# A selective-scan stage with whole scans in place of half scans, bf16 parts made ahead of their transfers, and another order in the experts' stage

## The reference, cut to what matters

```python
# experts, summed with the gate's weights w
h = relu(bn(einsum('bfd,edh->bfeh', x, W1) + b1)); h = relu(bn(einsum('bfeh,ehk->bfek', h, W2) + b2))
y = einsum('bfed,fe->bfd', einsum('bfeh,ehd->bfed', h, Wo) + bo, w)
# Mamba: 128 channels, 32 states for each channel, one step for each token
h = h * exp(dt_t[:, :, None] * A) + (dt_t * u_t)[:, :, None] * B_t[:, None, :]
y = einsum('bds,bs->bd', h, C_t)
```

## Time and profile before

| what | us |
|---|---|
| median of the timed runs (three, 1082.22 to 1087.21) | 1083.85 |
| the profiled execution's own time | 1080.03 |
| its span, first to last instruction | 1077.9 |
| PE, DVE, ACT, POOL busy in the span | 841.7, 799.9, 513.3, 541.9 |
| experts' stage, about 341.7 to 417 | 75 |
| scan stage, 499.5 to 965.1 | 465.6 |

### The profile page before, as it was taken

One profiled execution on the slowest core, in us unless ns is written; L12 is line 12 of the kernel. 1 busy time (PEld: TensorE's weight loads), 2 busy tenths in 40 slices (PEclk: granted clock), 3 DMA queues, 4 the chain that ended last, 5 costly groups with the idle time before them and its releaser, 6 DMA issues.

```text
span 1077.9 us, 11533 instructions
## 1 busy us (share of the span) xinstructions
PE 841.7 (78%) x3813; PEld 356.6 (33%) x3813; DVE 799.9 (74%) x1054; ACT 513.3 (48%) x1015; POOL 541.9 (50%) x356
## 2 busy tenths in 40 slices
PE   7873665768766997985897877887887887888897
PEld 4441344647634332431121111111111111114575
DVE  1249998866433333378999999999999999985465
ACT  1365300284352665574555555555554444436521
POOL 0010749410100000014999999999999999880100
PEclk9987855687565999895657578567567557559866
DMA  9000001600100000001110111011011011000001
GB/s 389 37 0 0 1 0 34 138 1 1 59 1 0 2 1 1 1 15 35 36 43 16 27 43 27 16 43 34 12 40 41 12 33 43 1 0 1 1 15 28
DMA packets 20505, 33.09 MB, mean 31 GB/s; under 512 B 10078, under 2 KB 19294, under 8 KB 19422
## 3 DMA queue, kind: packets, MB, share of 16 engines
q1 hardware_dynamic: 20446, 32.36, 10.6%
HBM read 17.57 MB, written 1.20 MB: 17 GB/s over the span
## 4 chain that ended last, share of the span: by engine, by line
PE 39%; DVE 31%; issue 13%; ACT 11%; POOL 4%; SPq 1%; DMA 1%; DVEq 0%; ACTq 0%; POOLq 0%
DVE pair_arrays L1617 13%; DVE pair_arrays L1601 5%; PE PS L748 4%; PE PS L720 4%; ACT pair_arrays L895 3%; PE PS L730 3%; PE PS L420 3%; PE PS L574 3%; ACT PS L895 3%; PE PS L840 2%; PE PS L510 2%; DVE pair_arrays L1423 2%; ACT token_weights L895 2%; PE PS L866 2%; PE PS L293 1%
## 5 line engine op out<-in xcount | busy, mean ns | idle before, releaser
L1257 POOL TENSOR_TENSOR pair_arrays<-pair_arrays 128x736 f32<-128x736 f32 x192 | 332.5, 1749 | 24.8 <-DVE pair_arrays L1617 24.5
L895 ACT ACTIVATE PS<-PS,A_negative 128x368 f32<-128x368 f32 x384 | 191.6, 538 | 129.6 <-PE PS L730 129.3
L1617 DVE TENSOR_TENSOR_SCAN pair_arrays<-PS,scan_carry,pair_arrays 128x368 f32<-128x368 f32 x256 | 235.8, 964 | 0.3
L1601 DVE TENSOR_TENSOR pair_arrays<-pair_arrays,PS 128x736 f32<-128x736 f32 x144 | 129.0, 896 | 8.8 <-PE PS L720 8.6
L748 PE MATMUL PS<-pair_arrays,weights 128*32 128x368 f32 x768 | 132.5, 715 | 1.5 <-POOL pair_arrays L1257 1.4
L1211 POOL TENSOR_TENSOR big<-pair_arrays 128x1104 f32<-128x1104 f32 (+15 forms) x32 | 55.8, 1762 | 131.5 <-DVE pair_arrays L1374 68.5
L1617 DVE TENSOR_TENSOR_SCAN pair_arrays<-PS,pair_arrays 128x368 f32<-128x368 f32 x128 | 110.3, 905 | 2.1 <-ACT PS L895 2.1
L720 PE MATMUL PS<-spread_rows,token_weights 96*128 96x368 bf16 x192 | 64.3, 428 | 37.9 <-DVE pair_arrays L1601 23.5
L1265 POOL TENSOR_TENSOR pair_arrays<-pair_arrays,token_weights 128x736 f32<-128x736 f32 x48 | 84.2, 1754 | 18.5 <-ACT token_weights L895 18.5
L720 PE MATMUL PS<-pair_arrays,token_weights 96*128 96x368 bf16 x192 | 71.7, 471 | 26.1 <-DVE pair_arrays L1601 19.8
L481 PE MATMUL PS<-big,weights 128*128 128x368 f32 (+15 forms) x192 | 62.8, 493 | 31.5 <-DVE big L1434 20.5
(11 more groups left out here) (190 smaller groups left out, 1246.3 us busy)
## 6 DMA issues: line engine op xcount, KB each, us to landing
big<-in_x SPq DMA_DIRECT2D x4, 2048.0 KB, 17.5
big<-decay_rows SPq DMA_DIRECT2D x4, 1104.0 KB, 15.7
spread_rows<-pair_arrays SPq DMA_DIRECT2D x96, 46.0 KB, 1.9
pair_arrays<-pair_arrays SPq DMA_DIRECT2D x96, 46.0 KB, 1.9
spread_rows<-big SPq DMA_DIRECT2D x48, 46.0 KB, 1.9
pair_arrays<-big SPq DMA_DIRECT2D x48, 46.0 KB, 1.9
weights<-in_wts SPq DMA_DIRECT2D x1, 2204.0 KB, 18.0
big<-in_wexp SPq DMA_DIRECT2D x1, 1536.0 KB, 7.6
```

Of the source, the lines that this page charges most:

```text
L895: return nc.scalar.activation(o, i, fn, **kw)
L1257: nc.gpsimd.tensor_tensor(hcbuf[t % NRING], hbuf[t % NRING], c4(seg).unsqueeze(1).to_broadcast([128, 2, G]), ALU.mult).then_inc(s("hc_read ...
L1601: tt(bx[t % NRING], b4(seg).unsqueeze(1).to_broadcast([128, 2, G]), PS[:, 2:4, 0:G], ALU.mult).then_inc(s("b_used"), 1)
L1617: nc.vector.tensor_tensor_scan(hbuf[t % NRING][:, h, :], PS[:, 4 + 2 * (t % 2) + h, 0:G], bx[t % NRING][:, h, :], carry[:, a:a + 1] if k e ...
```

## The change

**Parts.** ScalarE now makes the first bf16 part of each array (`first_part`) and the second from GpSimd's first remainder (`middle_part`); GpSimd writes the third as bf16 itself. The transfers copy bf16 rows, half the bytes, into one buffer that holds both segments' stacks, and the matmuls read them without a stride. SyncE waits for the four copies too.

**Scan.** One scan instruction does both halves of a step (`scan`). The 736 columns become 738: each half has a column ahead of it, in which the decay is 0 and the input is the carry, or 0. The halves lie next to each other across two banks (`decay_line`). The carry column is written by ScalarE (`carry_in`), two steps ahead. On VectorE the scan of step t - 1 comes behind the input product of step t. Eight small memsets clear the columns first.

**Experts.** TensorE does layer 1 of n + 1 ahead of layer 2 of n, and ScalarE the first activation of n + 1 ahead of the second of n.

```diff
-        stack = [[a.rearrange("p (j t) -> p j t", j=NJ) for a in two]
-                 for two in ((stack_own[:, 0], stack_own[:, 1]),
-                             (P1.rearrange("p a t -> p (a t)")[:, 0:NJ * G], P10.rearrange("p a t -> p (a t)")[:, 0:NJ * G]))]
+        stack = [[stack_own[:, a].bitcast(BF16)[:, i * NJ * G:(i + 1) * NJ * G].rearrange("p (j t) -> p j t", j=NJ)
+                  for a in range(2)] for i in range(2)]
...
+        def decay_line(t):
+            return PS[:, 4 + 2 * (t % 2):6 + 2 * (t % 2), :].rearrange("p b c -> p (b c)")[:, 512 - G1:512 + G1]
...
@@ SyncE
                 sp.wait_ge(s("rest_ready"), seg + 1)
+                sp.wait_ge(s("parts_moved"), 4 * (seg + 1))
...
-                    for part, rows in enumerate((at(1 + a, seg), rest[a][0], rest[a][1])):
+                    for part, rows in enumerate(parts16[a]):
@@ TensorE
             for n in range(NX):
+                if n + 1 < NX:
+                    layer1(n + 1)
                 layer2(n)
                 if n + 1 < NX:
-                    layer1(n + 1)
                     spread_weight(n + 1)
...
-                                            high(stack[seg % 2][1][0:3 * DB, 2 * (i % 2) + h]), start=True, stop=True)
+                                            stack[seg % 2][1][0:3 * DB, 2 * (i % 2) + h], start=True, stop=True)
@@ ScalarE
             for n in range(NG * E):
-                hidden2(n)
                 if n + 1 < NG * E:
                     hidden1(n + 1)
+                hidden2(n)
...
+            def first_part(seg, a):
+                if seg % B == 0:
+                    act.wait_ge(s("dt_ready"), seg // B + 1)
+                if seg:
+                    act.wait_ge(s(f"stack_in{(seg - 1) % 2}"), STACKED * ((seg - 1) // 2 + 1))
...
+                f(parts16[a][0], high(at(1 + a, seg)), ACT.Copy).then_inc(s("parts_moved"), 1)
+            def middle_part(seg, a):
+                act.wait_ge(s("rest_mid"), 2 * (seg + 1))
+                f(parts16[a][1], high(rest[a]), ACT.Copy).then_inc(s("parts_moved"), 1)
+            for a in (1, 0):
+                first_part(0, a)
+            for a in (1, 0):
+                middle_part(0, a)
             logarithms(NG - 1)
             square(NG - 1)
...
+            def carry_in(t):
+                b, i = t // NSTEP % B, t % NSTEP
+                act.wait_ge(s("carried"), t - B * NSTEP + 1)
+                act.wait_ge(s("scanned"), t - NRING + 1)
+                f(bfirst[t % NRING], carry[:, b * DS + 2 * i:b * DS + 2 * i + 2], ACT.Copy).then_inc(s("carry_put"), 1)
...
                 decay(t)
                 if 1 <= t <= CARRIED:
                     carry_on(t - 1)
+                if B * NSTEP <= t + 2 < NSEG * NSTEP:
+                    carry_in(t + 2)
+                if t // NSTEP < NSEG - 1 and 2 <= t % NSTEP <= 3:
+                    first_part(t // NSTEP + 1, 3 - t % NSTEP)
+                if t // NSTEP < NSEG - 1 and 4 <= t % NSTEP <= 5:
+                    middle_part(t // NSTEP + 1, 5 - t % NSTEP)
@@ VectorE
-            def scan_half(t, h):
...
-                dve.wait_ge(s("decay"), 2 * t + h + 1)
-                a = b * DS + 2 * i + h
-                nc.vector.tensor_tensor_scan(hbuf[t % NRING][:, h, :], PS[:, 4 + 2 * (t % 2) + h, 0:G], bx[t % NRING][:, h, :],
-                                             carry[:, a:a + 1] if k else 0.0, ALU.mult, ALU.add).then_inc(s("scanned"), 1)
+            def scan(t):
...
+                dve.wait_ge(s("decay"), 2 * t + 2)
+                nc.vector.tensor_tensor_scan(hline[t % NRING], decay_line(t), bline[t % NRING],
+                                             0.0, ALU.mult, ALU.add).then_inc(s("scanned"), 1)
...
             for t in range(NSEG * NSTEP):
-                if t:
-                    scan_half(t - 1, 0)
                 if not shared(t):
                     input_term(t)
                 if t:
-                    scan_half(t - 1, 1)
+                    scan(t - 1)
```

76 lines of the change are left out of this document (44 added, 32 removed).

## The result

| | before | after |
|---|---|---|
| median of the timed runs | 1083.96 us | 1106.24 us (1104.55 to 1106.71) |
| ratio to before | | 1.0207, 95% interval [1.0182, 1.0233] |
| profiled execution, span | 1077.9 us | 1104.8 us |
| experts, first activation to the sum behind the last | 75.2 us | 66.2 us |
| first scan to the end of the last | 465.6 us | 488.9 us |

What follows compares the result with a forecast made beforehand. VectorE was the first limit, GpSimd and TensorE close behind; afterwards a loop through TensorE bounds the scan stage. - 9.5 + 6.7 + 13.6 = + 10.8 us on 1080.0 gives 1090.8; timed runs lie 3.8 higher: 1095, range 1078 to 1108.

Steps and rivals of the forecast that it cites:

- Experts: Experts' stage: the new order cuts two experts from 5.58 to 4.65 us, a gain of 9.5 us, bounds 5 to 10.2.
- Start of the scan stage: Before the first scan step: SyncE's transfers wait for four ScalarE copies, + 6.7 us, bounds + 3 and + 7.5.
- Merged scan on VectorE: Scan stage: one 738-column scan takes 1.68 us, bounds 1.59 and 1.77, saving 23 us of VectorE's 456.
- rival D: Scan over two PSUM banks costs 1.77 us: 1099 us total; chance 0.72 together with the main forecast and two other rivals.
- 8 more: Scan stage's upper bound: + 8 us on top of + 25.9 if a scan takes 1.77 us.
- GpSimd's floor: Scan stage: GpSimd's own work, untouched by the change, is 451 us, or 37.6 us a segment.
- The loop: Scan stage: chain through TensorE closed by a whole scan takes 9.90 us for four steps, 40.96 a segment at lower clock.
- The clock: Scan stage: TensorE keeps its 29% share of the upper clock, so the stage takes 479.2 us, + 13.6.
- rival C: Scan stage: same loop, clock never rises, 1107 us total; chance 0.72 together with the main forecast and two other rivals.
- the other bound: Scan stage: upper bound of 491 us, towards which it tends if TensorE's longer waits release the upper clock less often.

Runs made afterwards that it cites:

- early_parts: Changed kernel with the first segment's four bf16 copies on ScalarE ahead of its last magnitude instead of behind it: 1100.01 us, ratio 1.0154 to the kernel before.
- y_later: Changed kernel with TensorE's y matmuls of a pair of steps moved behind the next odd step's input spreading: 1067.32 us, ratio 0.9859 to the kernel before.
- scan_first: Changed kernel with VectorE's scan of step t - 1 ahead of the input product of step t: 1114.99 us, ratio 1.0298 to the kernel before.
- y_one_early: Changed kernel with early ScalarE copies and one step's y matmuls behind every step's spreading: ratio 0.9842 to the kernel before; median of all ten runs 1081.2 us.
- the first dose: Changed kernel with the two input-spreading matmuls of every fourth step done twice: 1104.77 us, ratio 1.0200 to the kernel before.
- before_filled: Kernel before with five instead of two input-spreading matmuls every fourth step and one decay-spreading matmul repeated in odd steps: 1083.39 us, ratio 1.0004.
- padded_only: Kernel before with only three buffer rings' layout changed, halves 369 words apart instead of 368, one output-term buffer in token_weights: 1082.62 us, ratio 0.9997.

## Why the prediction was right and where it failed

**Experts: right.** - 9.5 forecast, - 9.0 in the trace, - 0.90% alone. Only ScalarE's wait was off: 0.5 us are left of it where I said under 0.2. My own sum had it: 4.65 us for two experts is a period of 2.33, and less the two activations (1.82) that is a wait of 0.5.

**Start of the scan stage: right.** + 6.7 forecast, + 5.7 between the two traces (from the end of the experts to the first product), + 0.62% alone, 6.2 us back by early_parts. The copies cost 0.45 each, not 0.4; the issue rate didn't change with the bytes.

**Merged scan on VectorE: right.** 1.68 forecast, 1.683 measured; rival D (1.77) falls. My bounds for D don't agree with each other: a scan of 1.77 costs the loop 0.09 us in each of 48 cycles, some 4 us and not "8 more". **GpSimd's floor** was too high, though nothing hung on it: its output term fell from 1.75 to 1.61 by the layout, which I took for nothing, and instructions in a row overlap, so that it was busy 441 us and not the 451 that I added up.

**The loop: right.** 9.90 forecast for four steps, 9.92 measured; 40.96 us a segment at the lower clock, and 488.9 / 12 = 40.7 measured. VectorE's idle time before its products is the 50 us or more that I named, and taking the y matmuls out of the chain (y_later) brought 36 us, some 27 of them at the same clock. So this chain bounds the changed kernel. My sums for other chains did worse: scan_first took longer than its sum at a higher clock, and y_one_early doesn't fit at all.

**The clock: wrong, and it is most of the error.** The step that failed is "I keep before's share of the upper clock: the loop's gaps on TensorE are much the same". I kept 29%; the stage has (0.51 - 0.5) / 0.5, some 2%. So it takes 488.9 us and not 479.2, which is 9.7 of the 11.5 us that the forecast fell short. With none of the upper clock, the sum is rival C's: 1107, measured 1106.2. That this agrees to 1 us is partly luck. The stage is 2.6 us shorter than C's 491.5, and two things that no term of mine had make up for it: the first scan now stands behind two products, 1.5 us later, and the code behind the stage took 1.2 more.

The gaps are the same only in sum: TensorE's busy time falls short of the stage by 79 us before and by 72 after. By half-microsecond windows, 45 of the 79 were at the upper clock, where TensorE is done early, and 32 lay in the 330 us at the lower one. After, nearly all of them, 68, are at the lower one. There the new loop takes 9.92 us for 8.5 of TensorE's work, so it breaks off three times in each cycle, where the loop before broke off twice. My own sum had this in it: a loop longer than TensorE's work at that clock is a gap in every cycle. I looked at the total and not at where the gaps fall. That more gaps as such hold the clock down is not shown, and the runs speak against it: the first dose has a smaller share of gaps at the lower clock than the kernel before (39 of 482 us against 32 of 330) and stays down, and scan_first has more (72 of 385) and rises.

The Trainium skill's TensorE: Matmul & The Clock Gate, Part 1, has activity release the lower level, and I gave what follows from that, 491, as the other bound. The trace agrees with that bound (488.9). What the runs add is that a load of 447 us in 489 doesn't release it here while breaks of 0.2 to 0.4 us stand in it, that 96 added matmuls that close two of the three breaks do, and that 9.8 us without any break may not (before_filled), so that the rule alone doesn't forecast the clock.

What stays open: what keeps the clock down in the changed kernel, since it rises behind one unbroken stretch and not behind another. In the kernel before it rose in a stretch that was unbroken from 775.87 to 781.23; after, TensorE was unbroken from 752.44 to 757.80, over the same D and y matmuls, and the clock stayed at 0.50. Nor is it shown what holds the repaired stage at 37.7 us a segment, where VectorE has 36.0 us of work.

The traces differ by 26.9 us and the medians by 22.3: some 4 us of the profiled execution after lie ahead of the experts, in code that the change doesn't touch.

## What to carry to other kernels

When a change lengthens a chain through TensorE until it bounds, the time begins to depend on TensorE's clock, and the share of the upper clock that the kernel had can't be carried over. Reckon the time with the lower clock throughout as well: here that was the answer, though in scan_first the clock rose in spite of a break in every cycle. Then take work out of that chain, by moving what has no hurry (here the y matmuls) to where another engine's latency is waited for; if nothing can be moved, a few matmuls done twice in the break may pay for themselves. And judge TensorE's order only together with the instructions of the engine that reads from it: the same move brought 3.4% with merged scans behind the product (0.9859 / 1.0207) and cost 3.1% with half-scans around it (1.0216 / 0.9910).

## What the hardware did that I had not expected

GpSimd's product of 128x736 takes 1.62 us in padded_only and 1.75 in the kernel before, with the same instructions: the halves of its operand lie 369 words apart instead of 368, and its buffers start elsewhere (which of the two does it isn't shown). The input term, which writes such a ring, stays at 1.75 in both. Repeating two matmuls in a break of TensorE's costs nothing (1104.8 against 1106.2 us, ratios 1.0200 [1.0183, 1.0218] and 1.0207 [1.0182, 1.0233]). A copy of 368 columns costs ScalarE 0.45 us and SyncE's issue 0.63 with 23 KB and 0.62 with 46.
